# Message passing by one-hot selection: one more step of 196 takes its rows from TensorE, and an early key row is made three steps later

## The reference, cut to what matters

```python
xn = (x - mean) * jax.lax.rsqrt(var + BN_EPS) * gamma + beta
xi = xn[dst]
xj = xn[src]
feat = jnp.concatenate([xi, xj - xi], axis=-1)
h = jax.nn.relu(feat @ W1 + b1)
msg = h @ W2 + b2
agg = jax.ops.segment_max(msg, dst, num_segments=N_NODES)
agg = jnp.where(jnp.isfinite(agg), agg, 0.0)
return jax.nn.relu(agg)          # then x = _layernorm(x + this)
```

## Time and profile before

| | |
|---|---|
| median of 3 runs | 2415.8 us (2410.23 to 2418.83) |
| profiled execution: its own time | 2424.7 us |
| its span, from the first to the last instruction | 2422.7 us |
| its mean granted TensorE clock | 0.878 |
| TensorE (PE) busy | 1818.5 us, 75% |
| VectorE (DVE) busy | 1292.7 us, 53% |
| ScalarE (ACT) busy | 862.0 us, 36% |
| GpSimd (POOL) busy | 1283.2 us, 53% |

### The profile page before, as it was taken

One profiled execution on the slowest core, in us unless ns is written; L12 is line 12 of the kernel. 1 busy time (PEld: TensorE's weight loads), 2 busy tenths in 40 slices (PEclk: granted clock), 3 DMA queues, 4 the chain that ended last, 5 costly groups with the idle time before them and its releaser, 6 DMA issues.

```text
span 2422.7 us, 31826 instructions
## 1 busy us (share of the span) xinstructions
PE 1818.5 (75%) x12305; PEld 938.5 (39%) x12305; DVE 1292.7 (53%) x2070; ACT 862.0 (36%) x968; POOL 1283.2 (53%) x1356
## 2 busy tenths in 40 slices
PE   2046887787878778787878878878788778887785
PEld 1032444343434434343434444444444434444443
DVE  2054655565555555555555556556456555565553
ACT  2044443333333333333333333333334333333333
POOL 7715245556555565456555565555655565555621
PEclk6557899998999999898989899998999988898996
DMA  4154223233333332333323333233323333333320
GB/s 93 35 173 122 59 84 81 77 90 86 80 86 84 88 95 70 85 81 96 87 70 91 87 87 80 81 89 95 89 72 94 91 81 81 75 94 87 76 62 5
DMA packets 132832, 202.31 MB, mean 84 GB/s; under 512 B 74828, under 2 KB 76937, under 8 KB 132648
## 3 DMA queue, kind: packets, MB, share of 16 engines
q0 software_dynamic: 43440, 85.03, 16.5%
q1 hardware_dynamic: 87946, 115.04, 14.9%
q10 hardware_dynamic: 1294, 0.20, 0.1%
HBM read 189.19 MB, written 12.60 MB: 83 GB/s over the span
## 4 chain that ended last, share of the span: by engine, by line
another core or an unknown queue 38%; PE 29%; ACT 19%; issue 8%; DVE 5%; DMA 1%; SPq 0%; POOLq 0%; DVEq 0%; ACTq 0%
PE ps_g L1146 10%; PE ps_g L1153 6%; ACT hid L688 5%; ACT best L640 5%; PE ps_mr L1190 4%; ACT best L644 4%; ACT best L683 3%; PE ps_acc L1234 2%; DVE oh L919 2%; PE ps_h L1205 2%; PE ps_mr L1196 2%; PE ps_h L1215 1%; DVE runmax L993 1%; PE ps_h L1222 1%
## 5 line engine op out<-in xcount | busy, mean ns | idle before, releaser
L511 POOL DMA_INDIRECT xb<-b_dram,src_ix x1248 | 1181.1, 946 | 1031.4 <-PE ps_h L1205 384.9
L919 DVE TENSOR_SCALAR oh<-ps_k 128x1024 bf16<-128x1024 bf16 x1372 | 849.6, 678 | 1.0
L1146 PE MATMUL ps_g<-oh,xtab 128*128 128x512 bf16 x2744 | 643.5, 387 | 5.8 <-issue 5.0
L1190 PE MATMUL ps_mr<-hid,w 128*64 128x512 f32 x784 | 270.8, 776 | 369.9 <-ACT best L683 325.6
L972 DVE TENSOR_TENSOR best<-ps_acc,last_key 128x336 f32<-128x336 f32 x196 | 99.3, 507 | 815.8 <-remote 655.9
L683 ACT ACTIVATE best<-ps_mr 128x512 f32<-128x512 f32 x196 | 117.0, 597 | 1097.1 <-remote 816.3
L1146 PEld LDWEIGHTS ps_g<-oh,xtab 128*128 128x128 bf16 x2744 | 256.9, 99 | 375.6 <-issue 103.3
L1153 PE MATMUL ps_g<-oh,xtab 128*64 128x512 bf16 x2744 | 387.1, 424 | 12.6 <-issue 11.3
L993 DVE TENSOR_TENSOR_SCAN runmax<-rb,runmax,ps_mr 128x512 f32<-128x512 bf16 x196 | 249.6, 1274 | 97.4 <-PE ps_mr L1190 55.1
L688 ACT ACTIVATE hid<-ps_h,bias 128x1024 f32<-128x1024 f32 x196 | 217.9, 1112 | 106.8 <-remote 42.2
L1190 PEld LDWEIGHTS ps_mr<-hid,w 128*64 128x64 f32 x784 | 44.1, 154 | 479.6 <-ACT best L683 391.8
(11 more groups left out here) (181 smaller groups left out, 537.2 us busy)
## 6 DMA issues: line engine op xcount, KB each, us to landing
kb<-keys_dram SPq DMA_DIRECT2D x98, 504.0 KB
rb<-reset_dram SPq DMA_DIRECT2D x98, 256.0 KB
xb<-b_dram,src_ix POOLq DMA_INDIRECT x1248
src_t<-in_src SPq DMA_DIRECT2D x56, 256.0 KB
aw<-a_dram SPq DMA_DIRECT2D x196, 31.5 KB
a_dram<-oh SPq DMA_DIRECT2D x6, 672.0 KB, 3.5
xwin<-xp_dram SPq DMA_DIRECT2D x196, 10.5 KB
out<-y SPq DMA_DIRECT2D x182, 10.5 KB
```

Of the source, the lines that this page charges most:

```text
L511: pool.indirect_dma_start(xb[:, u, t, h, :], None, b_dram[:, :], bass.IndirectOffsetOnAxis(ap=src_ix[:, b, q + t, h:h + 1], axis=0))\
L919: dve.tensor_scalar(oh[0:PN, n % NOH, :], node_keys_ps, n % TN + 0.5, None, ALU.is_equal).then_inc(oh_ready, 1)
L1146: last = pe.matmul(ps_g[:, h, :], xtab[0:PN, t, 0:2, :].rearrange("p w c -> p (w c)"), oh[0:PN, n % NOH, h * GE:(h + 1) * GE], start=t == ...
L1190: last = pe.matmul(ps_mr[h * C:(h + 1) * C, :], w2[:, :], hid[:, j % 2, h, :], start=True, stop=True)
```

## The change

Two numbers change. PICKED goes from 28 to 29, so 29 steps are picked and 155 instead of 156 are gathered in the wide way, and the planner spreads 29 sets of 49 tiles over the same 190 steps. And ACT makes the keys of the second set at the end of its step 4, not of its step 1.

```diff
@@ -48,7 +48,7 @@
     AS = 4
     NOH = 14
     AHEAD = 5
-    PICKED = 28
+    PICKED = 29
     REST = 8
@@ -707,7 +707,7 @@
                         window_onehot(k + 2)
                     for g in range(2 * k, min(2 * k + 2, XG)):
                         x_mid_piece(g)
-                    if segment < PICKED and k == first_step[segment - 1] + 1:
+                    if segment < PICKED and k == first_step[segment - 1] + (4 if segment == 1 else 1):
                         node_keys(segment)
                         segment += 1
```

## The result

| | before | after |
|---|---|---|
| median, 6 runs each on one chip | 2419.66 us (2410.23 to 2423.42) | 2448.06 us (2437.99 to 2450.99) |
| ratio, 95% interval | | 1.011 (1.0087 to 1.0133) |
| profiled execution: own time, span | 2424.7, 2422.7 us | 2450.99, 2449.1 us |

The account below looks back on a forecast made before the run. POOL's gathers were taken to pace gathered steps, TensorE's tiles picked ones. Gathered and short steps -10.2 us, picked steps +21, tiles elsewhere +2.0 gave +12.8, taken as +12 on 2415.8: 2428 us, range 2411 to 2441.

Parts of the forecast that it names:

- Gathered steps keep POOL's pace, and tiles beside them are hidden: Gathered steps: eight gathers plus some 2 us set 11.84 us each; 26 added tiles there cost nothing, at most 17 us.
- the hidden tiles are not hidden: Rival, gathered steps: the 26 added tiles cost 0.65 us each, so +12 becomes +29, 2445 us; chance 0.07.
- The eight ordinary steps that go, and the one behind a picked step: Gathered steps: eight ordinary ones fewer, -94.7 us; one more behind a picked step, +12.5 us.
- The three more short pairs at 24.0 us each: Short steps with the step behind each: three more pairs by the planner's table, +72.0 us.
- The row of the step of 20.80 us: Profile row of a step behind a short one, granted clock 0.75; cited for slow clock and for 9 tiles outlasting POOL.
- guess of 24 to 26 us for pairs that begin with a single tile: Expected sign in the changed profile: such pairs take 24 to 26 us, with stretches at a granted clock below 0.9.
- Picked steps: Picked steps, 237 instead of 217 tiles: +23.0 us by class means, less 2 for those without a short step ahead: +21.
- Tiles elsewhere: Three tiles added in early and late steps without a wide gather, at 0.65 us each: +2.0 us.
- One-hots: DVE makes 49 more of 678 ns, in all 33 us, but is five tiles ahead: no cost.
- Keys: ACT's keys row moved from step 1 to step 4, where ACT waits: taken as 0, bounds 1.1 us either way.
- No difference: Rival: picked steps average 8.6 to 9.1 us, giving -7 to +7 us, 2409 to 2423; chance 0.28.
- faster: Rival: picked steps run at their floor of 8.60, 8.00 and 7.30 us, sum -16, 2400 us; chance 0.08.

Follow-up runs that it names:

- e7: Changed kernel with the seven short steps of 1 or 2 tiles raised to 3, taken from the steps ahead: 2438.03 us, ratio 1.0048 to the kernel before.
- e5: Kernel before (28 picked, keys in step 1) with the other tiles of each set spread evenly, no short steps: 2397.17 us, ratio 0.9883.
- e3: Changed kernel (29 picked) with the other tiles of each set spread evenly, no short steps: 2411.2 us, ratio 0.9943 to the kernel before.
- e2: Changed kernel with PICKED back at 28, so only the keys moved to step 4: 2425.81 us, ratio 1.0007 to the kernel before.

## Why the prediction was wrong in size

The direction was right, and so was the pace of the gathered steps; the size was too small by 14 us (+12.8 by the sum, +26.4 by the two traces).

- **Gathered steps keep POOL's pace, and tiles beside them are hidden: right.** The tile matmuls alone of a step with 8, 7 and 9 tiles, in the changed kernel, as the earlier trace rows:

```profile
832.90:844.60 11.70, 3.63 (x16) 1.48 (x16) 0.74 0.18 48
844.60:856.40 11.80, 3.19 (x14) 1.29 (x14) 0.99 0.43 106
1984.50:1996.30 11.80, 4.06 (x18) 1.68 (x18) 0.86 0.20 54
```

  The rival "the hidden tiles are not hidden" gave 2445, near the measured time, by a mechanism that didn't happen: the ordinary steps keep 11.84 us.

  What the prediction did not ask is how the gathers hold a step up at all, for POOL works eight gathered steps, not eight single gathers, ahead: at 1036.17 to 1037.21, just before POOL's wait in the earlier trace rows ends, TensorE reads rows that were gathered from 930.51 to 940.20. The times of the semaphores in the trace of before show what comes late. TensorE's rows near the end of the step that ends at 1050.44 read

```profile
1045.28 0.60 PE L1196 MATMUL ps_mr<-ident,runmax 128*128 128x128 f32 x4
1045.71 1.04 PE L1205 MATMUL ps_h<-ident,xb 128*128 128x128 f32 x8
```

  but their signals, for which ACT, DVE and POOL wait, come at 1050.42 and 1050.51, behind the last gather's end at 1048.63. In 138 of the 148 gathered steps from 13 to 186 no gather is under way when the step ends; there the signal of `turn` comes 1.75 us behind the last gather's end (median), and in 128 of them over 1 us after the recorded end of the turned rows. At the end of the 26 picked steps in the same stretch it comes within 0.02 us of that end. The 120 waits of the earlier trace rows are waits for this signal. With six gathers it still comes 1.49 us behind the last one. Whether the signals are late or the matmuls' rows too early (their ends are modelled), and why only beside gathers, no run shows.
- **The eight ordinary steps that go, and the one behind a picked step: right** (-95.6 for -94.7, +13.8 for +12.5).
- **The three more short pairs at 24.0 us each: this is the step that failed.** The term was +72.0 and measured +86.4. The mean of 24.0 was taken from short steps with 2 to 6 tiles and applied to emptier ones, on the ground that POOL needs its time all the same and the next step pays a short one back. It does not where POOL's next eight follow without a pause: the three pairs with a single tile took 26.9 us on the mean. The row of the step of 20.80 us showed the stall that they suffer; I read it as a slow clock and as work that is paid back. With at least 3 tiles in every short step the mean was 24.0 (e7). The prediction's own guess of 24 to 26 us for pairs that begin with a single tile was not in its sum.
- **Picked steps: +21 predicted, +26.1 measured.** The means of the classes were 10.25, 8.57 and 7.70 us for 9, 8 and 7 tiles. Taking off 2 us for the steps without a short one two ahead was right for those (7.9, 7.9 and 8.2 us), but the 9-tile ones grew from 9.99 to 10.25. All 17 of these stand behind a short pair; without short steps they take 9.54. Why the picked step is longer there, beyond the two-step stall, was not taken apart. This miss is no larger than what two executions of one plan differ by: the kernels with one edit alone, with 28 and with 29 picked steps, have 244.8 and 258.5 us here where before and after have 239.1 and 265.2, a difference of 13.7 instead of 26.1. Their short pairs cost 484.3 and 567.8 us, +83.5, so the miss in the pairs stands.
- **Without the short steps' stall, the sum holds.** e5 against e3 gives 14 us for the 29th picked step, and the prediction's sum was 12.8, by nearly the same terms: picked steps +22.0 (+21 predicted), the step behind +12.6 (+12.5), the other gathered steps -19.8 (-94.7 + 72.0 = -22.7).
- **Tiles elsewhere, +2.0: not seen.** The steps at both ends give -4.4 instead. That is 6 us in the change's favour, which hides part of the miss; it was not taken apart, and the two traces are one execution each.
- **One-hots: right.** DVE idles 1.0 us ahead of them, as before.
- **Keys: no cost, right (e2), but their place was read wrongly.** I put them at some 249.5 us, ahead of a wait of 4.43. The row stands a step earlier:

```profile
237.07 1.13 ACT L633 ACTIVATE best<-src_t,node 128x1024 bf16<-128x1024 int32 x1
...
253.00 0.60 ACT L683 ACTIVATE best<-ps_mr 128x512 f32<-128x512 f32 x1 [4.43 <-PE ps_mr L1196]
```

- **"No difference" and "faster"** would have needed picked steps of 9.1 us or less on the mean. They took 265.2 / 28 = 9.47.

**What stays open.** Shown is when TensorE stalls: POOL issues 16 gathers without a pause, and matmuls whose one-hots are long made start one by one until about 3 us after the last gather. That TensorE's signals come late beside eight gathers too suggests one cause for both; this is argued, not shown. Not shown is what TensorE lacks then. The profile names nothing, no run changed it by itself, and nothing here tells a shared path of instructions or signals from an effect of the gathers' writes. Nor was a version tried in which POOL is held back for a pause of 2 us, which would be the direct test.

## What to carry to other kernels

When work is spread by an even progress and cut at set boundaries, look at the smallest piece it leaves: a mean price of "short" steps does not hold for emptier ones, and one odd row in the group (here 20.80 us beside a mean of 14) is the one to follow. Work that is hidden beside a fixed pace belongs there, and not in steps where it counts: with 28 picked steps, doing without short steps brought 1.2% and moving tiles out of the picked steps another 2.7 points, where one picked step more cost 1.1%. Look for the best count again when the distribution has changed: 28 picked steps beat 29 with and without short steps, and with the picked ones emptied 27 beat both (27 was not tried with full ones).

## What the hardware showed that I had not expected

- Eight gathers of 128 rows take 9.70 us on POOL, also in the stretches where TensorE stalls, and the pause behind them belongs to the step: in ordinary steps 2.09 us with eight gathers and 1.87 with six (medians). It does not wait for the rows just gathered, which TensorE reads eight gathered steps later, but for a signal of TensorE that comes 1.75 us behind the last gather.
- Perfetto Trace Analysis of the Trainium skill, "DMA Instruction — SWDGE (GPSIMD)", says that a gather's row ends when the descriptors are made and not when the data has moved. The trace agrees: the eight gathers that follow those of the earlier trace rows end at 1048.63 by POOL's rows, and their signals of landing come until 1050.90.
- Where gathers were issued 2 us earlier, two steps were 3 us longer: without the pause between two sets of eight the pair takes 26.2 to 27.7 us (16 places in 14 traces), with it 23.3 to 24.4 (21 pairs in three).
- TensorE's matmuls can be 1.4 to 2.3 us apart and 0.39 to 0.59 us long, their idle time named issue, while POOL gathers 16 times in a row. Usual are 0.24 us apart (13 in 3.15 us, at the lower clock).
